# Convolution on eight PE array tiles without a halo transfer, and the mean taken out by PE

## The reference, cut to what matters

```python
# gx: (256, 16, 128, 128), normalized x
gap, gmp = mean(gx, (2, 3)), max(gx, (2, 3))
channel_weight = sigmoid(gn(conv1x1(concat(gap, gmp), w_cc, b_cc)))
x_h, x_w = mean(gx, 3), mean(gx, 2)              # row means, column means
hw = conv1x1(concat(x_h, x_w), w_s1, b_s1)
pos_h, pos_w = sigmoid(conv1x1(hw[:h])), sigmoid(conv1x1(hw[h:]))
sx = conv3x3(gx * pos_h * pos_w, w_s3) + b_s3    # 16 -> 16 channels
spatial_weight = sigmoid(gn(sx))                 # over 128 x 128 pixels
out = x + gx * (channel_weight * spatial_weight)
```

## Time and profile before

| | us |
|---|---|
| three runs, median (lowest, highest) | 4297.4 (4295.71, 4300.11) |
| the profiled execution, its time | 4296.2 |
| its span, first to last instruction | 4294.3 |
| PE busy | 4041.4 (94%) |
| VectorE (DVE) busy | 4018.4 (94%) |
| ScalarE (ACT) busy | 2624.4 (61%) |
| GpSimd (POOL) busy | 1775.4 (41%) |
| DMA | 728.87 MB, 74.7% of 16 engines' span |
| mean granted clock of PE | 0.965 |

### The profile page before, as it was taken

How to read it: one execution, slowest core, us unless ns; L and a number is a source line. 1 busy time by engine, 2 the same in 40 slices (tenths; PEclk the granted TensorE clock), 3 DMA queues, 4 the chain that set the end, 5 groups by cost and what they waited for, 6 DMA issues and landing times.

```text
span 4294.3 us, 55492 instructions
## 1 busy us (share of the span) xinstructions
PE 4041.4 (94%) x11016; PEld 1938.2 (45%) x11016; DVE 4018.4 (94%) x2719; ACT 2624.4 (61%) x4354; POOL 1775.4 (41%) x2314
## 2 busy tenths in 40 slices
PE   5999999999999999999999999999999999999997
PEld 2444444444444444444444444444444444444443
DVE  7999999999999999999999999999999999999996
ACT  3566566666665666666656666666666666665665
POOL 3443444444434434443344434344444344434443
PEclk9999999999999999999999999999999999999998
DMA  6777777777777777777777777777777777777775
GB/s 124 163 173 173 172 175 169 175 172 173 172 173 169 177 173 172 175 167 178 172 172 172 172 176 172 171 172 176 168 177 173 172 175 167 177 173 173 171 177 123
DMA packets 1147751, 730.57 MB, mean 170 GB/s; under 512 B 74144, under 2 KB 1122976, under 8 KB 1147552
## 3 DMA queue, kind: packets, MB, share of 16 engines
q1 hardware_dynamic: 1147552, 728.87, 74.7%
HBM read 268.64 MB, written 268.44 MB: 125 GB/s over the span
## 4 chain that ended last, share of the span: by engine, by line
DVE 53%; issue 18%; SPq 11%; DMA 9%; PE 6%; POOL 1%; ACT 1%; DVEq 1%; POOLq 0%; ACTq 0%
DVE sums L560 13%; DVE mx L607 12%; SPq L222 11%; DMA xt<-in_x 9%; DVE sp_buf L524 7%; DVE sums L554 7%; DVE gated L567 7%; DVE sp_buf L527 6%; PE conv_ps L637 5%; POOL rstd L275 1%; ACT sp_buf L416 1%; DVE gate_hr L594 0%; PE pos_ps L637 0%; DVE ch L603 0%; DVE sums_n L545 0%
## 5 line engine op out<-in xcount | busy, mean ns | idle before, releaser
L637 PE MATMUL conv_ps<-gated,W_conv 128*128 128x512 f32 x6144 | 2973.1, 619 | 16.5 <-DVE gated L567 16.3
L637 PEld LDWEIGHTS conv_ps<-gated,W_conv 128*128 128x128 f32 x6144 | 1143.4, 197 | 1100.0 <-issue 1071.7
L637 PE MATMUL conv_ps<-halo,W_halo 96*128 96x512 f32 x2048 | 1027.7, 604 | 2.1 <-DMA halo<-gated 1.6
L370 ACT ACTIVATE sp_buf<-conv_ps,weights 128x1024 f32<-128x1024 f32 x512 | 565.3, 1104 | 747.8 <-PE conv_ps L637 747.5
L323 POOL TENSOR_TENSOR gated<-gate_w,gate_hr 128x2048 f32<-128x2048 f32 x256 | 918.7, 3609 | 166.9 <-DVE gate_hr L594 157.6
L560 DVE TENSOR_REDUCE sums<-xt 128x128 f32<-128x2048 f32 x256 | 943.6, 3725 | 0.0
L554 DVE TENSOR_REDUCE sums<-xt 128x16 f32<-128x2048 f32 x256 | 584.2, 2282 | 171.5 <-DMA xt<-in_x 171.4
L524 DVE SCALAR_TENSOR_TENSOR sp_buf<-xt,negm,sp_buf 128x2048 f32<-128x2048 f32 x256 | 600.6, 2346 | 38.3 <-ACT sp_buf L416 38.3
L527 DVE SCALAR_TENSOR_TENSOR sp_buf<-sp_buf,kfac,xt 128x2048 f32<-128x2048 f32 x256 | 602.1, 2352 | 9.0
L567 DVE SCALAR_TENSOR_TENSOR gated<-xt,negm,gated 128x2048 f32<-128x2048 f32 x256 | 593.9, 2361 | 0.0
L343 POOL TENSOR_TENSOR rstd<-var_e,consts 128x2 f32<-128x2 f32 x128 | 89.8, 701 | 1176.8 <-DVE var_e L581 1176.8
(11 more groups left out here) (79 smaller groups left out, 2174.4 us busy)
## 6 DMA issues: line engine op xcount, KB each, us to landing
xt<-in_x SPq DMA_DIRECT2D x2048, 128.0 KB, 3.0
out<-sp_buf SPq DMA_DIRECT2D x2048, 128.0 KB, 2.5
halo<-gated SPq DMA_DIRECT2D x512, 365.2 KB, 6.0
weights<-in_by_channel SPq DMA_DIRECT2D x1, 116.5 KB, 2.6
S_chan<-in_same_channel SPq DMA_DIRECT2D x1, 64.0 KB, 1.9
whalo_in<-in_wconv SPq DMA_DIRECT2D x2, 3.0 KB, 1.8
masks<-in_row_masks SPq DMA_DIRECT2D x1, 12.0 KB, 1.9
hmask<-in_halo_mask SPq DMA_DIRECT2D x1, 3.0 KB, 1.9
```

The lines of the kernel that those rows point to most:

```text
L370: nc.scalar.activation(sp_buf[:, g, k * 8:k * 8 + 8], conv_ps[:, h % 2], ACT.Identity, bias=V["b_s3"], accum_out=ssum2[:, g, k:k + 1]).the ...
L637: return nc.tensor.matmul(ps, lhsT, rhs, start=start, stop=stop)
```

## The change

1. Partitions are numbered anew: partition `32 (r // 2) + 2 c + r % 2` holds channel `c`, row `r`, so that a quarter of 32 partitions has two neighbouring rows of all 16 channels. Loads and stores use `row_partitions(r)`, again 16 partitions each, with a step of 2 in place of 8. The weights are expanded in quarters, 68 linked VectorE operations in place of 24 ahead of the first product on PE, and `by_channel` comes already repeated.
2. `halo`, `W_halo`, `halo_rows` and their transfers go. `gated` gets an empty band at each end ([NB + 2] bands), and `row_masks` wraps around.
3. The convolution of one PSUM bank (four bands) uses eight tiles of the array, 64 rows by 32 columns. Upper half of the partitions (rows 0 to 3) and lower half (rows 4 to 7) are separate contractions, and each output quarter (a pair of rows) has its own matmul. The pair (0, 1) reads the lower half from one band before, the pair (6, 7) reads the upper half from one band after. In slot `n` the upper tiles of bank `n` and the lower tiles of bank `n - 1` alternate, one kernel column at a time, so the lower half of a unit's last bank falls in slot 0 of the next turn.
4. The convolution uses four banks in turn, ScalarE evacuates one bank (512 columns) at a time, eight per unit.
5. `sums_n` goes. `positions` multiplies the raw sums with scaled weights and adds the mean in two more products with a broadcast operand. Column sums go to `col_sums`, by the same strided reduction.
6. The small products stand elsewhere between the pieces of the convolution (below).

```diff
-        gated = sb("gated", [P, 2, 2, NB, WP])
-        halo = sb("halo", [HALO, 2, 2, NB * WP])
+        gated = sb("gated", [P, 2, 2, NB + 2, WP])
...
+        def row_partitions(r):
+            at = QUAD * (r // 2) + r % 2
+            return slice(at, QUAD * (r // 2 + 1), 2)
...
-                            sp.dma_start(xt[r:P:RB, vs, j], come[r]).then_inc(x_in[vs][j], 16)
+                            sp.dma_start(xt[row_partitions(r), vs, j], come[r]).then_inc(x_in[vs][j], 16)
...
                 load(0)
                 store(0)
-                halo_rows(0)
-                halo_rows(1)
                 load(1)
                 store(1)
...
-                nc.scalar.activation(sp_buf[:, g, k * 8:k * 8 + 8], conv_ps[:, h % 2], ACT.Identity,
+                nc.scalar.activation(sp_buf[:, g, k * BB:(k + 1) * BB], conv_ps[:, k], ACT.Identity,
                                      bias=V["b_s3"], accum_out=ssum2[:, g, k:k + 1]).then_inc(evac, 1)
...
-            for s in range(2):
-                for col in (0, WP - 1):
-                    link(nc.vector.memset(gated[:, s, :, :, col:col + 1], 0.0))
+            link(nc.vector.memset(gated[:].rearrange("p s j b w -> p (s j b w)"), 0.0))
...
-                    for j in range(2):
-                        nc.vector.tensor_scalar(sums_n[:, da, j, 0:NB], sums[:, da, j, 0:NB], 1.0 / W,
-                                                negm[:, sa, j:j + 1], ALU.mult, ALU.add)
-                        ins = nc.vector.tensor_scalar(sums_n[:, da, j, NB:], sums[:, da, j, NB:], 1.0 / NB,
-                                                      negm[:, sa, j:j + 1], ALU.mult, ALU.add)
-                    ins.then_inc(sn_done, 1)
...
                 def positions():
                     if real(a):
-                        pe.wait_ge(sn_done, a + 1)
+                        pe.wait_ge(sums_done, 2 * a + 2)
+                        pe.wait_ge(cols_done, 2 * a + 2)
+                        pe.wait_ge(negm_done, a + 1)
                         if later(a, 1):
                             pe.wait_ge(gates_done, 4 * a)
-                        mm(pos[:, :, 0:NB], W_rows[:, :], sums_n[:, da, :, 0:NB])
-                        mm(pos[:, :, NB:NB + W], W_cols[:, :], sums_n[:, da, :, NB:]).then_inc(pos_mm, 1)
+                        shift = negm[:, sa].unsqueeze(2)
+                        mm(pos[:, :, 0:NB], W_rows[:, :], sums[:, da], stop=False)
+                        mm(pos[:, :, 0:NB], W_rows_m[:, :], shift.to_broadcast([P, 2, NB]), start=False)
+                        mm(pos[:, :, NB:NB + W], W_cols[:, :], col_sums[:, da], stop=False)
+                        mm(pos[:, :, NB:NB + W], W_cols_m[:, :], shift.to_broadcast([P, 2, W]),
+                           start=False).then_inc(pos_mm, 1)
...
+                def tiles(u, d, n, half, kw, start):
+
+                    j, k = n // BANKS, n % BANKS
+                    for o in range(PAIRS):
+                        band = 1 + BB * k
+                        if half == 1 and o == 0:
+                            band -= 1
+                        if half == 0 and o == PAIRS - 1:
+                            band += 1
+                        rows = slice(ROW_TILE * half, ROW_TILE * (half + 1))
+                        cols = slice(QUAD * o, QUAD * (o + 1))
+                        ins = mm(conv_ps[cols, k], W_conv[rows, kw, cols],
+                                 gated[rows, d, j, band:band + BB, kw:kw + W], start=start and kw == 0,
+                                 stop=not start and kw == KW - 1)
+                    return ins
+
+                def slot(n, first=0, last=KW):
+
+                    if real(t) and first == 0:
+                        if n % BANKS == 0:
+                            pe.wait_ge(mod_done, 2 * t + n // BANKS + 1)
+                        if later(8 * t + n, BANKS):
+                            pe.wait_ge(evac, 8 * t + n - BANKS + 1)
+                        pe.sem_inc(bank_free, 1)
+                    for kw in range(first, last):
+                        if real(t):
+                            ins = tiles(t, q % 2, n, 0, kw, True)
+                            if kw == KW - 1:
+                                ins.then_inc(upper_mm, 1)
+                        if real(t) if n > 0 else real(b):
+                            if kw == 0:
+                                pe.wait_ge(upper_mm, 8 * t + n)
+                                pe.sem_inc(upper_ready, 1)
+                            if n > 0:
+                                ins = tiles(t, q % 2, n - 1, 1, kw, False)
+                            else:
+                                ins = tiles(b, sb_ % 2, 7, 1, kw, False)
+                            if kw == KW - 1:
+                                ins.then_inc(conv_mm, 1)
 
                 mean()
-                conv(0, 0, 2)
                 maxima()
...
+                slot(0)
+                slot(1)
                 mean2(b, sb_, 1)
+                positions()
+                slot(2)
+                slot(3, 0, 1)
                 variance()
+                channel()
+                slot(3, 1, KW)
+                slot(4)
                 var2(b, sb_, 1)
+                slot(5)
                 mean2(t, q, 0)
+                slot(6)
+                slot(7)
                 var2(t, q, 0)
```

More of the change, by code:

```diff
@@ L73, in conv_attention @@
         S_chan = sb("S_chan", [P, P])
[L75 to L76 removed]
+        sums = sb("sums", [P, 2, 2, NB])
+        col_sums = sb("col_sums", [P, 2, 2, W])
+        W_rows_m = sb("W_rows_m", [P, P])
+        W_cols_m = sb("W_cols_m", [P, P])
         tot = sb("tot", [P, 2, 2])
```

192 lines of the change are left out of this document (69 added, 123 removed).

## The result

The changed kernel took 5315.94 us (median of 4 runs, 5313.43 to 5316.19) against 4296.56 (4294.99 to 4300.11) for the kernel before on the same chip: a ratio of 1.237, 95% interval 1.2348 to 1.2391. The forecast was 4198 us, its range 4110 to 4480. The kernel became a quarter slower.

The account below looks back on a forecast made before the run. The prediction took a ring of VectorE work, SyncE issue and load landing (32.7 us a turn) as the bound. From 4296.2 us it took 99 (124 turns x 0.8), added 0 for both ends and 1: about 4198 us, range 4110 to 4480.

Parts of the forecast that it names:

- The bound: Whole turn of the kernel before: paced by VectorE work and the input load, 32.7 us, with PE outside.
- ring of `load(1)`: VectorE and SyncE, each turn: 24.0 us of VectorE, 0.2 to wake SyncE, 8.5 of issue and landing, together 32.7.
- Waits that move: PE to GpSimd after earlier channel products: gate products at +14.5 to +21.7 from VectorE's turn start, 4 to 5 us cover.
- waits behind the channel products: Rival: with slots of 2.9 or more and low clock, VectorE waits 1 to 3 us a turn; 4230 to 4500; chance 0.06.
- The convolution on tiles: PE: eight tiles all at once, 24 steps of 0.86 us, 20.6 us per turn, a slot of 2.58.
- passes in order: Rival on PE: each tile matmul costs one 0.43 us step, turn about 87, total near 11,000 us; chance 0.12.
- issue-bound tiles: Rival on PE: 0.07 us per load-and-pass pair, convolution 26.9 us, PE the bound; 4395, up to 4480 us; chance 0.16.
- serial rival: Rival on PE, same as passes in order: tile matmuls one after another, total near 11,000 us; chance 0.12.
- The halo's removal: SyncE's loads: without four halo issues per turn, the turn falls from 33.00 to 32.2 us.
- 0.57 and 0.25: Input load, per turn: 0.57 us saved from late turns, 0.25 from earlier landing in ordinary turns (bounds 0 and 0.5).
- `sums_n` at nothing: VectorE: four operations of 0.67 us go, costed at nothing because row sums just wait 0.67 longer for the load.
- Small terms: ScalarE: eight evacuations instead of four pairs cost 1.8 us more per turn, hidden on an engine at 61%.

Follow-up runs that it names:

- e11: Kernel before, with only VectorE's order changed: second row-sum reduction and `tot` moved behind the first column sum; 4106.1 us.
- e5: Changed kernel, PE does `variance` before slot 3, `var2` after it, channel products after slot 4; GpSimd's group 0 gate product ahead of `rstd2(b, 1)`; 4318.4 us.
- e2: Changed kernel, only GpSimd's order altered: gate product of group 0 ahead of `rstd2(b, 1)` of the unit before; 4446.1 us.
- e9: e5 with the convolution as 24 full-array matmuls per turn instead of tiles, leaving out rows across a band's edge; 4207.0 us.
- e10: e5 plus VectorE's second row-sum reduction and `tot` moved behind the first column sum; 4128.9 us.
- e12: e10 with the convolution as 24 full-array matmuls per turn instead of tiles, leaving out rows across a band's edge; 4008.1 us.

## Why the prediction was wrong, point by point

**The bound (right).** The ring of `load(1)` did pace the kernel before: e11 opens it without any other change and gains 191 us. In e5, where the order is mended, it is the bound again.

**Waits that move (the step that failed).** The prediction followed the move as far as the gate products, "+14.5 to +21.7", saw 4 to 5 us of cover and stopped. Two instructions of GpSimd come behind them, `channel_norm` and `rstd2(t, 0)`, and the second holds ScalarE's sigmoid, the last evacuations and with them `mean2` and PE. The prediction gave `channel_norm` no line and thereby its usual 2.9 us. It measured 10.88. PE's wait for `gmx_n` came as forecast (1.61 us here) and was nearly harmless in itself, for e2 keeps it; it pushed the gate products to the place where `channel_norm` meets VectorE's modulation. The two stretches at the lower clock came as well, near the 2 us each that the prediction allowed; it took them as covered, but once the ring of waits sets the turn nothing covers them. The kernel before already held the hint, in `kfac`, of the same size as the operations of `channel_norm` (minimum, median and maximum in ns):

```profile
L336 POOL TENSOR_TENSOR kfac<-cgate,rstd x128: 194/1142/2268, 50.1 to 4247.0; 128x2 f32<-128x2 f32 x128
```

Its mean there is 1288 ns. It was not read.

**The rival "waits behind the channel products"** had the right place and the wrong price: 1 to 3 us a turn with a slot of 2.9. The mechanism was not a late gate product but a held small operation behind it, 8 us, with slots of 2.81.

**The convolution on tiles (nearly right).** 20.6 us for 24 steps, a slot of 2.58, was forecast; the slot is 2.81 at full clock and the turn's convolution 8 x 2.81 = 22.5. Neither "passes in order" nor "issue-bound tiles" came. The Trainium skill, "TensorE: Matmul & The Clock Gate" (Part 3, The mechanism), says that matmuls start and end strictly in program order, and the prediction took that to mean the serial rival at 11,000 us. It does not follow: matmuls that start in order can still overlap, and here eight tiles' passes lie in one step of 0.43 us.

**The halo's removal (the second miss).** 32.2 us was forecast as 33.00 less 0.57 and 0.25. The landing did shrink, from a median of 2.9 us to 2.6 in e5 (200 to 4150 us), and e9, without the halo and without the tiles, shows a turn of 32.24 and 4207 us, close to the 4198 of the sum. (The 0.57 rests on nineteen turns; the 86 ordinary turns between 200 and 4000 us have a mean of 32.53, which makes it 0.48.) But that holds only without the tile program, and e9 also leaves out work on PE that a right result needs. With the tiles (e5) the gain is given back: long issues and longer column sums bring the turn to 33.11. PE's stops are there too, 111.0 us in 29, but VectorE's wait behind them is 8.5 us in e5: they cost only where the ring of `load(1)` is open. The term missing from the sum is what a long PE program costs its neighbours: 52,488 executed matmul passes against 11,016.

**`sums_n` at nothing (right while the load was last).** VectorE's wait for the input rose from 155.8 us before to 205.8 in e5, with `sums_n` gone and the turn no shorter.

**Small terms.** ScalarE's eight evacuations last 0.675 + 0.19 us on average, 6.9 us a turn against 5.2 before, close to the 1.8 more that were forecast. Hidden they were not in the changed kernel: two of them stand in its ring, with 1.65 us.

## What to carry to other kernels

When an instruction moves, follow its engine's queue to the end of the turn, not to the first instruction with cover, and price each small operation by what the other engine is doing at its new place. A tiny GpSimd operation whose mean stands far above its minimum (1288 against 194 ns) is a sign that it is held: look for what VectorE runs beside it, and place such operations beside reductions. And before giving a loaded engine less to do, ask whether the late load is needed where it stands; here one reordering on VectorE was worth more than the whole redesign.

## What the runs showed of the hardware that was not expected

- GpSimd's operations on two elements lasted 2.1 to 2.8 us beside VectorE's two-input operations over 2048 elements, 1.05 to 1.12 beside a `tensor_scalar` of 1.24, and 0.20 beside reductions. VectorE's `maxima_in` was held for 1.99 instead of 0.17 by GpSimd's gate product.
- Tiles of 64 rows by 32 columns ran eight at a time in float32: 48 passes in 2.81 us.
- With 52,488 matmul passes in the run PE stops for 3.5 to 4.3 us once per loop of four turns in e10; with 9,480 in e12 it does not. With the stops came longer column sums on VectorE, 3.86 us against 3.69, and long issues on SyncE: 184 of 1,941 load issues over 0.7 us in e10, 2 of 1,936 in e12. In the changed kernel itself, where PE waits more, the column sums are 3.77 and the stops 1.8 to 2.3. Why the tile program reaches VectorE and SyncE was not settled.
